# Sliding-window attention on one core: GpSimd's order around the masking, ScalarE's small copies and TensorE's table of scores, maxima and sums

## What is computed

```python
q = (x @ Wq.T) ...; k = (x @ Wk.T) ...; v = (x @ Wv.T) ...      # 16 heads of 16 features
attend = abs(i - j) <= 128 or i < 1 or j < 1                    # window, and one global token
logits = where(attend, q @ k.T / 4, -inf)
out = softmax(logits) @ v;  x = x + out @ Wo.T
```

## Time and profile before

| | before |
|---|---|
| device time, median of 3 runs | 1068.22 us (1067.39 to 1068.65) |
| the profiled execution: device time | 1071.5 us |
| its span | 1068.9 us |
| mean granted TensorE clock | 0.995 |
| busy: TensorE, VectorE, ScalarE, GpSimd | 97%, 86%, 73%, 65% |
| HBM traffic | 130 GB/s over the span |

### The profile page before, as it was taken

The page is one execution under the profiler, slowest core; times in us unless marked ns, Lnnn a source line. Parts: engine busy times, 40 slices in busy tenths (PEclk is TensorE's granted clock), DMA queues, the critical chain, the costliest instruction groups (busy, mean ns, idle before and its releaser), DMA issues.

```text
span 1068.9 us, 40083 instructions
## 1 busy us (share of the span) xinstructions
PE 1031.5 (97%) x16071; PEld 789.2 (74%) x16071; DVE 921.4 (86%) x3202; ACT 775.2 (73%) x1328; POOL 699.6 (65%) x945
## 2 busy tenths in 40 slices
PE   9999999799999999999999999999999999999997
PEld 8888887466665666557665666588888888888886
DVE  7889987799999999999999999487888888888885
ACT  7989987687888888887888878854566554556554
POOL 3575556688888888898888888843344443344443
PEclk9999999899999999999999999999999999999999
DMA  6999989878667766776677653512122221123001
GB/s 210 263 314 276 286 231 267 155 136 154 129 139 156 157 126 137 158 145 130 139 138 160 131 120 70 143 38 80 59 89 90 60 60 60 60 79 95 26 21 40
DMA packets 187019, 142.33 MB, mean 133 GB/s; under 512 B 61625, under 2 KB 186577, under 8 KB 186833
## 3 DMA queue, kind: packets, MB, share of 16 engines
q1 hardware_dynamic: 186832, 139.77, 55.3%
HBM read 87.98 MB, written 50.95 MB: 130 GB/s over the span
## 4 chain that ended last, share of the span: by engine, by line
PE 60%; DVE 11%; issue 4%; SPq 3%; ACT 2%; DMA 1%; POOL 0%; DVEq 0%; ACTq 0%
PE e_psum L1616 13%; PE e_psum L1638 12%; PE e_psum L1347 9%; PE e_psum L1906 6%; PE e_psum L1908 6%; DVE a_masked L1362 4%; PE e_psum L1888 3%; PE e_psum L1887 3%; DVE n_stats L144 2%; DVE f_x L2028 2%; SPq L1321 2%; PE e_psum L231 1%; PE e_psum L233 1%; PE e_psum L232 1%; PE e_psum L1892 1%
## 5 line engine op out<-in xcount | busy, mean ns | idle before, releaser
L1692 ACT ACTIVATE a_weights<-e_psum 128x1024 f32<-128x1024 f32 (+1 forms) x512 | 391.4, 809 | 85.2 <-PE e_psum L1616 84.7
L1362 DVE CUSTOM_DVE_ANT_0 a_masked<-e_psum,band 128x290 f32<-128x290 f32 (+1 forms) x992 | 387.7, 445 | 37.9 <-PE e_psum L1347 32.1
L1526 POOL TENSOR_SCALAR_AFFINE_SELECT a_weights<-a_weights 128x1024 f32<-128x1024 f32 x256 | 273.9, 1094 | 48.6 <-ACT a_weights L1692 47.2
L1950 POOL TENSOR_TENSOR f_square<-f_relu 128x512 f32<-128x512 f32 x128 | 147.6, 1154 | 212.8 <-ACT f_relu L1939 189.6
L1347 PE MATMUL e_psum<-e_k,e_q 96*32 96x290 bf16 (+2 forms) x4096 | 236.5, 287 | 15.6 <-DVE max L1362 6.5
L1616 PE MATMUL e_psum<-e_q,e_k 128*32 128x384 bf16 (+2 forms) x5632 | 241.6, 280 | 5.8 <-ACT a_weights L1692 3.6
L1638 PE MATMUL e_psum<-a_weights,a_v 128*17 128x384 f32 (+2 forms) x2816 | 221.7, 389 | 2.0 <-issue 1.4
L1616 PEld LDWEIGHTS e_psum<-e_q,e_k 128*32 128x32 bf16 x5632 | 132.0, 96 | 97.0 <-ACT a_weights L1692 40.9
L1347 PEld LDWEIGHTS e_psum<-e_k,e_q 96*32 96x32 bf16 x4096 | 116.8, 97 | 84.1 <-DVE max L1362 46.7
L1906 PE MATMUL e_psum<-w_w_t,f_square_hi 128*128 128x256 f32 x512 | 129.4, 287 | 4.6 <-DVE f_square_lo L2004 4.6
L1939 ACT ACTIVATE f_relu<-e_psum,w_mag 128x512 f32<-128x512 f32 x128 | 87.4, 683 | 54.5 <-PE e_psum L1892 54.5
(11 more groups left out here) (215 smaller groups left out, 1925.3 us busy)
## 6 DMA issues: line engine op xcount, KB each, us to landing
k_parts<-p_k_parts SPq DMA_DIRECT2D x48, 258.0 KB, 4.7
q_parts<-p_q_parts SPq DMA_DIRECT2D x48, 256.0 KB, 5.5
e_q<-q_parts SPq DMA_DIRECT2D x64, 192.0 KB, 4.0
e_k<-k_parts SPq DMA_DIRECT2D x60, 193.5 KB, 3.7
v_ones<-p_va SPq DMA_DIRECT2D x16, 544.0 KB, 5.9
p_x<-in_x SPq DMA_DIRECT2D x16, 512.0 KB, 7.0
e_q<-q_parts SPq DMA_DIRECT2D x64, 128.0 KB, 3.9
f_o<-attention SPq DMA_DIRECT2D x16, 512.0 KB, 4.7
```

The costliest lines, as they stand in the source:

```text
L1362: dve.tensor_tensor_reduce(out=masked[:, place + lo:place + hi], in0=bank[:, lo:hi], in1=self.band[:, lo:hi], scale=1.0, scalar=NEG, op0=A ...
L1526: pool.affine_select(out=blocks, in_=blocks, compare_op=ALU.is_ge, fill=0.0, base=0, pattern=[[0, NQ // 2 * HEAD_COLS // P // CUT_STEP], [ ...
L1692: act.activation(pe_w[:, us.upar, lo:hi], score[c % 2][:], ACT.Exp).then_inc(s_exp, 1)
L1950: pool.tensor_tensor(sh.r2[:, j % 4, :], sh.r[:, j % 4, :], sh.r[:, j % 4, :], ALU.mult).then_inc(self.s_sq, 1)
```

## The change

It edits only orders; no instruction is added or removed and none has another shape.

- **GpSimd.** The cuts of a unit's second half leave the end of the unit's own step and come at the start of the next. In a pair step the rest (`max_rest`) stands ahead of them, and the low part between the two. The global key's difference and the numerator and denominator come behind them (numerator first), then the cuts of the first half, and the global key's product behind those.
- **ScalarE.** The copy of the middle part comes behind E0, where it came behind E2; the exponential of the global key behind E5, where it came behind E7.
- **VectorE.** The reciprocal stands behind tile 9, where it stood behind tile 11.
- **TensorE.** The table is another: S0 S1 t0 t1 t2 S2 t3 t4 S3 S4 t5 t6 S5 t7 t8 Σ0 S6 S7 t9 t10 Σ1 Σ2 S8 t11 t12 Σ3 S9 S10 t13 S11 t14 t15 Σ4 Σ5.

```diff
 AFTER_TILE = (
-    (), (("score", 2),), (), (), (("score", 3), ("score", 4), ("score", 5)),
...
+    (), (), (("score", 2),), (), (("score", 3), ("score", 4)), (), (("score", 5),), (),
...
@@ GpSimd
             def body(at):
-                um, us, uo = at(L_SHIFT), at(L_SCORE), at(L_OUT)
+                um, us, up, uo = at(L_SHIFT), at(L_SCORE), at(L_SUM), at(L_OUT)
                 if um and um.last:
                     pool.wait_ge(s_high, um.pair + 1)
                     wait(pool, s_low, um.pair)
                     pool.tensor_tensor(rest[:], mt[:], shift[:, um.ppar, HIGH, :], ALU.subtract).then_inc(s_rest, 1)
+                if up and up.n < UNITS - 1:
+                    cut(up, 1, 0)
+                if um and um.last:
+                    pool.wait_ge(s_mid, um.pair + 1)
+                    pool.tensor_tensor(shift[:, um.ppar, LOW, :], rest[:], shift[:, um.ppar, MID, :], ALU.subtract
+                                       ).then_inc(s_low, 1)
+                if up and up.n < UNITS - 1:
+                    cut(up, 1, 1)
+                if um and um.n >= 2:
+                    wait(pool, s_p0, um.n - 1)
+                    sh.pool_key0(pool, um, masked)
...
-                if us and us.n < UNITS - 1:
-                    cut(us, 1, 0)
-                    cut(us, 1, 1)
@@ ScalarE
-                    if um and um.last and c == 2:
+                    if um and um.last and c == 0:
                         act.wait_ge(s_rest, um.pair + 1)
                         act.activation(shift[:, um.ppar, MID, :], rest[:], ACT.Copy).then_inc(s_mid, 1)
-                    if um and um.n and c == CHUNKS - 1:
+                    if um and um.n and c == 5:
@@ VectorE
-                    if uo and (ux or uo.n == UNITS - 2) and j == 11:
+                    if uo and (ux or uo.n == UNITS - 2) and j == 9:
                         sh.dve_denominators(dve, uo)
```

More of the change, by code:

```diff
@@ L936 @@
 AFTER_TILE = (
-    (), (("score", 2),), (), (), (("score", 3), ("score", 4), ("score", 5)),
-    (), (), (("sum", 0),), (("score", 6), ("score", 7), ("sum", 1)),
-    (), (("sum", 2),), (("score", 8), ("score", 9), ("score", 10)),
-    (), (), (("sum", 3), ("score", 11), ("sum", 4)), (("sum", 5),))
+    (), (), (("score", 2),), (), (("score", 3), ("score", 4)), (), (("score", 5),), (),
+    (("sum", 0), ("score", 6), ("score", 7)), (), (("sum", 1), ("sum", 2), ("score", 8)), (),
+    (("sum", 3), ("score", 9), ("score", 10)), (("score", 11),), (), (("sum", 4), ("sum", 5)))
 def in_group(gi, kb):
@@ L1535, in body @@
                     pool.tensor_tensor(rest[:], mt[:], shift[:, um.ppar, HIGH, :], ALU.subtract).then_inc(s_rest, 1)
+                if up and up.n < UNITS - 1:
[9 more added lines that the diff above has]
+                    sh.pool_key0(pool, um, masked)
+                if uo:
+                    pool.wait_ge(s_turned, uo.n + 1)
+                    pool.tensor_tensor(num[:, uo.upar], turned[:, uo.upar, :, 0:HD], t0[:, uo.n % 3], ALU.add
+                                       ).then_inc(s_num, 1)
                 if uo:
@@ L1539, in body @@
                                        ).then_inc(s_den, 1)
[L1540 to L1545, removed]
+                if us:
+                    cut(us, 0, 0)
+                    cut(us, 0, 1)
+                if us and us.n == UNITS - 1:
+                    cut(us, 1, 0)
+                    cut(us, 1, 1)
                 if us:
```

## The result

| | before | changed |
|---|---|---|
| device time, median of 4 runs on one chip | 1068.43 us (1067.39 to 1069.48) | 1077.31 us (1074.99 to 1079.36) |
| the profiled execution: device time, span | 1071.5, 1068.9 us | 1074.99, 1073.3 us |
| mean granted TensorE clock | 0.995 | 0.995 |

What follows compares the result with a forecast made beforehand. A step was taken as 1.74 us to S3, then TensorE's unbroken 6.0. Step terms of 11.6, scaled to 10.5, less 2.9 gave +7.6, rounded to +7: 1075 us, range 1071 to 1079 (8 in 10: 1060 to 1082).

Steps and rivals of the forecast that it cites:

- The mechanism: TensorE waits ahead of t8 and, in pair steps, Σ0: middle-group steps 7.85 us for 7.75, pair steps 8.08 for 7.74.
- The sum: Whole kernel: step terms of 11.6 us, scaled to 10.5, less 2.9 for row transfers: +7.6, rounded down to +7.
- t8 waits for tile 4: TensorE ahead of Σ0, every step: t8 waits until VectorE has read tile 4, a new hole of 0.17 us.
- The hole at S5: TensorE behind S3, every step: S5's wait for E1, 0.07 us, goes when S5 moves behind t5 and t6.
- The cuts behind the shift: GpSimd, pair steps: rest at 0.68 behind S0, second cut delays Σ0 to 3.3; step 8.08 us, +0.34.
- The row transfers: SyncE's three transfers leave about 1.7 us earlier, removing all TensorE waits for `e_q<-a_shift`: -2.9 us.
- The middle copy costs nothing: ScalarE ahead of E1: delays it about 0.12 us, hidden since S5 needs E1 only at 2.42; otherwise S5 would wait.
- Faster: Rival: VectorE sets the step and ends earlier; with tile 4 and cuts in time, 1061 us; chance 0.28.
- No change: Rival: waits at t8 and Σ0 fall into time already lost, row transfers pay the rest: 1068 us; chance 0.12.
- Slower by more through the reciprocal: Rival: GpSimd sets pair steps, late reciprocal stops VectorE at tile 10, some 0.3 us more each: 1084 us; chance 0.1.
- TensorE's weight loads against VectorE: In the profile's window TensorE's weight loads fill 19.84 of 31 us, 64%, where VectorE has 93%.

Runs made afterwards that it cites:

- e1_table_only: The kernel before with only the changed TensorE table, engine orders of GpSimd, ScalarE and VectorE as before: 1074.22 us, ratio 1.0058.
- e2_orders_only: The changed kernel with the TensorE table of before, so only the new orders of GpSimd, ScalarE and VectorE: 1084.59 us, ratio 1.0164.
- e3_cut_first: The changed kernel with GpSimd's first cut ahead of the rest of the maxima, the second behind it ahead of the low part: 1070.92 us, ratio 1.0030.
- e5_both: The changed kernel with GpSimd's first cut ahead of the rest, and Σ0 behind t7 with t8 behind it: 1065.01 us, ratio 0.9954.
- e6_t9_too: e3_cut_first with Σ0, S6 and S7 moved behind t9, which waits for tile 5: 1083.24 us, ratio 1.0138.
- e9_s5_later: The kernel before with one table edit, S5 behind t5 and t6: 1067.43 us, ratio 0.9977.
- e11_s5_cut_first: e3_cut_first with the table of before, except S5 behind t5 and t6: 1064.47 us, ratio 0.9963.
- e8_old_table_cut_first: e3_cut_first with the TensorE table of before: 1069.77 us, ratio 1.0014.
- e10_middle_late: e8_old_table_cut_first with ScalarE's middle copy back behind E2, where it was before: 1070.66 us, ratio 1.0020.

## Why the prediction was right, point by point

**The mechanism** was right. In the middle groups (32 of 64 steps; medians of 16 plain and 16 pair steps of each profile, us) Σ0's distance from S0 and the step's length are:

| | Σ0, plain step | Σ0, pair step | plain step | pair step |
|---|---|---|---|---|
| before | 2.84 | 2.83 | 7.74 | 7.77 |
| changed | 3.08 | 3.30 | 7.86 | 8.10 |
| `e1_table_only` | 3.08 | 3.08 | 7.86 | 7.86 |
| `e2_orders_only` | 2.83 | 3.45 | 7.74 | 8.38 |
| `e3_cut_first` | 3.07 | 3.12 | 7.86 | 7.86 |
| `e5_both` | 2.79 | 2.87 | 7.70 | 7.72 |
| `e6_t9_too` | 3.45 | 3.46 | 8.11 | 8.11 |

The table alone lengthens both kinds of step by the same wait, the orders alone lengthen the pair steps and no others, and one cut moved takes the pair step's surplus away.

**The sum** was right in sign and nearly in size (+7 forecast, +8.9 measured). Its parts can be read from all groups' steps. This is the median plain step plus the median pair step, by the group's place in its batch (6 to 8 steps of each kind; the first and last two units, where the pipeline fills and drains, left out):

| | first | second | third | last |
|---|---|---|---|---|
| before | 15.22 | 15.59 | 15.31 | 15.11 |
| changed | 15.37 | 15.86 | 15.88 | 15.46 |
| `e1_table_only` | 15.19 | 15.67 | 15.65 | 15.01 |
| `e3_cut_first` | 15.09 | 15.72 | 15.75 | 15.00 |
| `e5_both` | 14.73 | 15.47 | 15.41 | 14.79 |

The change adds 0.15, 0.27, 0.57 and 0.35, where 0.37, 0.44, 0.44 and 0.20 were forecast: too much for the first half of a batch, too little for the rest. In the last groups the forecast let t8 find tile 4 read in every step. The narrow tiles (162 to 258 columns for t0 to t3) stand in the last three steps of such a group and in the first of the next batch, since the maxima are made three units ahead of the scores. The plain step that has them went from 7.49 to 7.37, the one that doesn't from 7.45 to 7.62. Eight pairs of each give 10.7 us, where 11.6 were said. The table's part is 2.4 us (`e1_table_only` less before; 1.9 by the forecast's terms, if t8's price falls on both steps of a pair), that of the cuts 8.1 (changed less `e3_cut_first`; forecast 11.6 less 1.9), that of t8 in the good order 9.3 (`e3_cut_first` less `e5_both`; 0.17 in 48 steps is 8.2). The ratios of whole runs give another split of the same total: the table 6, the cuts 5 to 6, the transfers (`e3_cut_first` less `e1_table_only`) -3, each such difference uncertain by some 3 us. The parts are therefore known to a few us only, and that 7 came so near to 8.9 is in part luck: the errors by group (0.22 and 0.17 too much, 0.13 and 0.15 too little a pair) cancel, and no run resolves the 2.9 of the transfers. The table's two values, 2.4 and 6, differ most; see what stays open.

**t8 waits for tile 4**: confirmed at 0.16 (0.17 forecast) and by `e5_both` and `e6_t9_too`. **The hole at S5** was mis-sized: 0.07 in each of 64 steps is 4.5 us, and `e9_s5_later`, which closes it alone, gave 2.5 (its interval reaches from 0.9 to 4.1). In its middle groups Σ0 comes 0.06 earlier in plain steps but only 0.02 in pair steps (2.78 and 2.81 behind S0).

**The cuts behind the shift**: confirmed step by step (rest 0.68 forecast, 0.70 measured; Σ0 3.3 and 3.30), and in a full pair step 8.11 where 8.08 was said.

**The row transfers**: the mechanism is confirmed, its price is not resolved. The wait's row is gone in the changed kernel and is still 2.6 us in 7 places in `e1_table_only`. By whole runs `e3_cut_first` is 3 us faster than that kernel and `e11_s5_cut_first` 1.5 us faster against its own baseline than `e9_s5_later`, each uncertain by 2 to 3 us; `e8_old_table_cut_first` ended 1.5 over before with 3.7 lost at S5. That points to 2 or 3 us. The medians of the steps don't show it, since it falls on few of them.

**The middle copy costs nothing**: true of this table only. With S5 where it was it costs 0.12 in each pair step (`e8_old_table_cut_first`), the condition that the prediction named.

**The rivals.** Faster: fell. TensorE doesn't find tile 4 read: VectorE starts it 2.42 to 2.43 behind S0 in the median step, before and changed alike, in plain steps. VectorE's smaller share (27.74 of 31 us for 28.80) isn't relief, since its work is the same and the steps are longer. No change: fell. Slower by more through the reciprocal: fell. GpSimd ends the denominator at 504.71, and VectorE makes the reciprocal at 505.52, right behind tile 9, with no wait for it:

```profile
504.48 0.23 POOL L1552 TENSOR_TENSOR e_den<-e_turned,e_p 128x16 f32<-128x16 f32 x1
```
```profile
505.52 0.25 DVE L1413 RECIPROCAL e_rden<-e_den 128x16 f32<-128x16 f32 x1
```

**TensorE's weight loads against VectorE.** With weight loads in 64% of the window and VectorE busy in 93%, order alone moves the time: `e6_t9_too` changes nobody's work and loses 0.25 us a step to one wait of TensorE (8.11 for 7.86), and `e5_both` gains with VectorE's work unchanged. The wait at t8 is for VectorE's read, though, and no run here made that work shorter; what a shorter one would give isn't shown.

**What stays open.** Executions of one kernel scatter by 8 to 9 us (`e1_table_only` 1067.67 to 1075.34, `e10_middle_late` 1068.21 to 1077.32). The profile of `e1_table_only` is the fastest of its executions, so that it doesn't show the 6 us of the whole runs. One contribution can be seen in TensorE's matmuls that wait with no releaser, 190 to 700 us, in `e3_cut_first`:

```profile
PE e_psum L1639 <- issue: 3.9, 6, 1.2
PE e_psum L1617 <- issue: 1.2, 2, 1.0
```

In the profile of the changed kernel these rows add up to 0.2 us, in that of before to 3.1. Without them the way from the first turning to the last is 483.1 us before (486.2 - 3.1), 492.7 changed, 487.2 in `e3_cut_first` (492.3 - 5.1): the same order as the medians. These rows don't cover all of it: in the profile before, single steps of middle groups take up to 8.41 us where 7.74 is usual. What the stalls are wasn't found.

## What to carry to other kernels

Where an engine's queue is in order (in the step shown GpSimd's two cuts were ready 0.43 us before the rest ahead of them could start) and each of its steps waits once, what counts is the place of each wait and the work that stands between it and the wait before; follow one step from engine to engine with durations from the timeline, and the length of the new step comes out to 0.03 us (7.85 and 8.08 forecast, 7.86 and 8.10 measured in the middle groups), while shares of busy time say nothing (TensorE has 97% in both kernels). Two instructions that are ready shouldn't queue behind one that waits for three engines: the same GpSimd work with one cut ahead of the rest fills the wait and still sends the rows early. And a change made of several reorderings is to be taken apart: here two parts gained (S5 later, the rows sent early) and two lost more, and moving one cut and one block of sums turned 8.9 us slower into 4 to 5 faster.

## What the runs showed of the hardware that was not expected

The cost of two waits isn't their sum: TensorE's table cost 6 us and the other engines' orders 17 alone, 9 together. In a pair step t8's wait for VectorE (until about 2.95 behind S0) lies inside Σ0's for GpSimd (until 3.30), and the new table also has the maxima turned 0.15 earlier. An instruction of 128x32 elements on ScalarE, 0.22 us by its record, delays S5, which waits for the exponential behind it, by 0.12 only (S3 to S5 0.83 for 0.71 in `e8_old_table_cut_first`).
